# Attention context computed transposed, with the softmax division on the probabilities, in a fused layer on one core

## The reference

```python
q = split_heads(x @ wq + bq); k = split_heads(x @ wk + bk); v = split_heads(x @ wv + bv)
scores = jnp.einsum('bhqd,bhkd->bhqk', q, k) * dh ** -0.5 + attn_bias[:, None, :, :]
attn = jax.nn.softmax(scores, axis=-1)
ctx = jnp.einsum('bhij,bhjd->bhid', attn, v)          # 128 x 48 for each of 8 heads
attn_out = ctx.transpose(0, 2, 1, 3).reshape(b, n, d) @ wo + bo
x = _rmsnorm(x + attn_out, alpha1, gamma1)
x = _rmsnorm(x + silu(x @ w1 + b1) @ w2 + b2, alpha2, gamma2)
```

## Time and profile before

| What | Value |
|---|---|
| Median of 3 runs | 3255.15 us |
| Span of the profiled execution | 3262.2 us |
| TensorE matmul busy | 2983.9 us (91%) |
| TensorE weight loads busy | 2873.5 us (88%) |
| VectorE busy | 1913.3 us (59%) |
| ScalarE busy | 1531.1 us (47%) |
| GpSimd busy | 1444.8 us (44%) |
| Granted TensorE clock, mean | 0.970 |

### The profile page before, as it was taken

The page is one execution under the profiler, slowest core; times in us unless marked ns, Lnnn a source line. Parts: engine busy times, 40 slices in busy tenths (PEclk is TensorE's granted clock), DMA queues, the critical chain, the costliest instruction groups (busy, mean ns, idle before and its releaser), DMA issues. The chain is left out here.

```text
span 3262.2 us, 63713 instructions
## 1 busy us (share of the span) xinstructions
PE 2983.9 (91%) x21571; PEld 2873.5 (88%) x21571; DVE 1913.3 (59%) x3165; ACT 1531.1 (47%) x3966; POOL 1444.8 (44%) x1406
## 2 busy tenths in 40 slices
PE   3999999999999999999999847788899999999986
PEld 2899999999999999999999836688799999999982
DVE  4456556565656565565656447445577766666754
ACT  3454545545454545454454434355544544444530
POOL 0334444443434343444444347200377766666750
PEclk9999999999999999999999969889999999999999
DMA  3000101010101011010101057455566666666869
GB/s 122 28 23 31 36 24 43 24 43 24 43 24 43 23 35 32 24 43 24 43 24 39 20 209 282 137 154 164 185 209 215 210 187 186 210 194 189 260 225 365
DMA packets 293646, 358.96 MB, mean 110 GB/s; under 512 B 24328, under 2 KB 285960, under 8 KB 293512
## 3 DMA queue, kind: packets, MB, share of 16 engines
q1 hardware_dynamic: 284840, 344.92, 33.0%
q10 hardware_dynamic: 8704, 12.58, 1.0%
HBM read 286.14 MB, written 71.30 MB: 110 GB/s over the span
## 5 line engine op out<-in xcount | busy, mean ns | idle before, releaser
L1607 PE MATMUL u_bank<-x_in,x_w 128*128 128x256 f32 x4608 | 584.1, 286 | 25.1 <-issue 19.5
L1607 PEld LDWEIGHTS u_bank<-x_in,x_w 128*128 128x128 f32 x4608 | 578.5, 195 | 26.5 <-issue 26.5
L925 POOL TENSOR_TENSOR hT_lo<-h_tmp,hT_hi 128x512 fp32r<-128x512 f32 x192 | 247.8, 1290 | 483.3 <-DVE hT_hi L813 483.3
L1760 POOL TENSOR_TENSOR x_w<-raw,x_w 128x768 fp32r<-128x768 f32 x128 | 274.0, 2141 | 297.3 <-DVE x_w L1703 297.3
L1764 POOL TENSOR_TENSOR x_aT<-x_act,x_aT 128x512 fp32r<-128x512 f32 x128 | 299.5, 2339 | 212.0 <-ACT x_aT L1672 212.0
L389 PE MATMUL m_bank<-yT_hi,w_hi 128*128 128x256 f32 x1152 | 339.9, 295 | 0.0
L1663 ACT ACTIVATE x_gelu<-u_bank,x_b1T 128x256 f32<-128x256 f32 x256 | 121.9, 476 | 439.3 <-PE u_bank L1607 439.3
L389 PE MATMUL m_bank<-yT_lo,w_hi 128*128 128x256 f32 x1152 | 324.5, 282 | 0.0
L389 PE MATMUL m_bank<-yT_hi,w_lo 128*128 128x256 f32 x1152 | 323.9, 281 | 0.0
L660 ACT ACTIVATE h_tmp<-m_bank,b1c 128x256 f32<-128x256 f32 x384 | 160.9, 470 | 330.2 <-PE m_bank L389 329.8
L1619 PE MATMUL o_bank<-x_w,x_aT 128*128 128x384 f32 x1536 | 287.9, 335 | 1.8 <-POOL x_aT L1764 1.8
(11 more groups left out here) (212 smaller groups left out, 7408.8 us busy)
## 6 DMA issues: line engine op xcount, KB each, us to landing
raw<-in_L_ffn_w_dram SPq DMA_DIRECT2D x384, 384.0 KB, 5.1
ws_raw<-in_L_ffn_w_slot_dram SPq DMA_DIRECT2D x8, 2304.0 KB, 9.6
x_in<-in_x_dram SPq DMA_DIRECT2D x32, 384.0 KB, 3.4
x_res<-in_x_dram SPq DMA_DIRECT2D x32, 384.0 KB, 4.1
residual<-f_sb SPq DMA_DIRECT2D x32, 384.0 KB, 2.5
yn<-yn_sb SPq DMA_DIRECT2D x32, 384.0 KB, 2.5
yk<-yn SPq DMA_DIRECT2D x16, 768.0 KB, 11.2
se<-se SPq DMA_DIRECT2D x16, 768.0 KB, 3.3
```

Of the source, the lines that this page charges most:

```text
L925: nc.gpsimd.tensor_tensor(hT[i % 3][1][:], h_tmp[i % 2][:], hT[i % 3][0][:].bitcast(F32), ALU.subtract).then_inc(hl.sem, 1)
L1607: mm = pe.matmul(u_bank[n % BANKS][:, g, :], w1s[i % 2][a][:, c, g, c2 * P:(c2 + 1) * P], xT[e % 2][b][:, c, :], start=c == 0 and j == 0, ...
L1760: nc.gpsimd.tensor_tensor(w2s[i % 2][1][:], raw2[i][:], w2s[i % 2][0][:].bitcast(F32), ALU.subtract).then_inc(w2_lo.sem, 1)
```

## The change

Context is computed transposed. For each head the weights are now the head's values, padded with zeros from 48 to 64 columns (`v_sb` becomes `[P, GT, H, HP]`), and the probabilities in `pT` are streamed, 128 columns. The result of a head of par 0 goes to partitions 0 to 63 of the bank, that of par 1 to 64 to 127, and the two are issued in turn. The bank then already holds the transposed context, in four blocks of 128 padded rows. `context_T`, `ctx_sb` and VectorE's `context` are gone. `wo` is laid out to match (four chunks with zero rows), so `project_out` issues 12 matmuls in place of 9, and `cT` has 512 columns in place of 384.

The division is now made on the probabilities: VectorE `normalise` multiplies the 1024 columns of `s_sb[t]` by the reciprocals in place, and `prob_T` waits for that (`pn_ok`) in place of the exponentials.

`comb` becomes the same memory as `logit`, and so ScalarE's `comb_exp` also waits for `logits_T`. Scratch outputs of the squares move into other tiles. The bank uses are renumbered (20 in place of 22). TensorE now issues `project_out(a,0)` right behind `up(m,2)`, then `context(a,1)`, `up(m,3)`, `weights_T`. VectorE issues the statistics of the next group ahead of `recips` and `normalise`, and `row_max` behind them.

```diff
-    wo_s = split_pair("wo", [P, DC, D])
+    wo_s = split_pair("wo", [P, H // 2, D])
...
+            elif i == 3:
+                flat = s[:, 0:H // 2 * D]
+                srcs = [(flat[HP * par:HP * par + DH, :].rearrange("p (m f) -> p m f", f=D),
+                         w.rearrange("(m two e) f -> two e m f", two=2, e=DH)[par]) for par in range(2)]
...
+                    if i == 3:
+                        sp.wait_ge(zeroed.sem, 3)
...
+                nc.vector.memset(stage[3][:], 0.0).then_inc(zeroed.sem, 1)
...
-    comb = t_sb("comb", [P, GT, P])
+    comb = logit
...
             def prob_T(g, t):
+                pe.wait_ge(pn_ok.sem, pn_ok.at(g, t + 1))
                 for par in range(2):
-                    pe.wait_ge(p_ok.sem, p_ok.at(g, 8 * t + 4 * (par + 1)))
...
             def context(g, t):
                 pe.wait_ge(v_ok.sem, v_ok.at(g, t + 1))
-                held, k = ((sc_ok, 4), (pt_ok, 3))[t]
-                pe.wait_ge(held.sem, held.at(g, k))
+                if t == 0:
+                    pe.wait_ge(sc_ok.sem, sc_ok.at(g, 4))
+                pe.wait_ge(pt_ok.sem, pt_ok.at(g, 2 * t + 2))
                 bank = A_BANK[U_CTX[t]]
-                for par in range(2):
-                    pe.wait_ge(pt_ok.sem, pt_ok.at(g, 2 * t + par + 1))
-                    for m in range(H // 2):
-                        h = 2 * m + par
-                        mm = pe.matmul(bank[:, h * DH:(h + 1) * DH], pT[:, par, m, :],
-                                       v_sb[:, t, h * DH:(h + 1) * DH], start=True, stop=True)
-                mm.then_inc(a_full.sem, 1)
+                for m in range(H // 2):
+                    for par in range(2):
+                        mm = pe.matmul(bank[par * HP:(par + 1) * HP, tok(m)], v_sb[:, t, 2 * m + par, :],
+                                       pT[:, par, m, :], start=True, stop=True)
                 mm.then_inc(a_full.sem, 1)
...
             def project_out(g, t):
                 pe.wait_ge(cl.sem, cl.at(g, t + 1))
...
+                split_mm(bank[:, 0:D], [[cT[s][:, c, :] for s in range(2)] for c in range(H // 2)],
+                         [[wo_s[s][:, c, :] for s in range(2)] for c in range(H // 2)]).then_inc(a_full.sem, 1)
...
                 if M: up(m, 2)
-                if A: context_T(a, 0); context(a, 1)
+                if A: project_out(a, 0); context(a, 1)
                 if M: up(m, 3)
-                if A: project_out(a, 0); context_T(a, 1)
                 if R: weights_T(r)
...
+            def hi_cT(g, t):
+                act.wait_ge(a_full.sem, a_full.at(g, U_CTX[t] + 1))
+                nc.scalar.copy(cT[0][:], A_BANK[U_CTX[t]][:].rearrange("p (c n) -> p c n", n=P)).then_inc(ch.sem, 1)
...
             def comb_exp(g):
                 act.wait_ge(lm_ok.sem, lm_ok.at(g, 1))
+                act.wait_ge(r_full.sem, r_full.at(g, 4))
...
-                if A: hi_T(a, 0, U_CT, cT[0][:], ch)
-                if M: silu(m, 2); silu(m, 3)
-                if A: hi_T(a, 1, U_CT, cT[0][:], ch)
+                if A: hi_cT(a, 0)
+                if M: silu(m, 2)
+                if A: hi_cT(a, 1)
+                if M: silu(m, 3)
...
+            def lo_cT(g, t):
+                dve.wait_ge(ch.sem, ch.at(g, t + 1))
+                nc.vector.tensor_tensor(cT[1][:], A_BANK[U_CTX[t]][:].rearrange("p (c n) -> p c n", n=P),
+                                        cT[0][:].bitcast(F32), ALU.subtract).then_inc(cl.sem, 1)
...
+            def normalise(g, t):
                 dve.wait_ge(rs_ok.sem, rs_ok.at(g, t + 1))
...
+                rows_of = s_sb[t][:].rearrange("p a m n -> p (a m) n")
+                nc.vector.tensor_tensor(rows_of, rows_of, rsum[:, t, :].unsqueeze(2).broadcast_to([P, H, P]),
+                                        ALU.mult).then_inc(pn_ok.sem, 1)
...
-                if A: values(a, 0); values(a, 1); scores(a, 0); scores(a, 1); recips(a, 0)
+                if A: values(a, 0); values(a, 1); scores(a, 0); scores(a, 1)
                 if N: norm_stats(n, x_landed, 16, x_in, st, mv, stats, meanvar)
-                if R: row_max(r)
-                if A: context(a, 0); recips(a, 1)
-                if R: slot_max(r); comb_norm(r)
-                if A: lo_T(a, 0, U_CT, cT[0][:], cT[1][:], ch, cl)
+                if A: recips(a, 0); normalise(a, 0); recips(a, 1); normalise(a, 1)
+                if R: row_max(r); slot_max(r); comb_norm(r)
+                if A: lo_cT(a, 0)
                 if R: disp_recip(r)
                 if M: h_hi(m, 2)
-                if A: context(a, 1)
+                if A: residual(a, 0); lo_cT(a, 1)
                 if M: h_hi(m, 3)
-                if A: residual(a, 0); lo_T(a, 1, U_CT, cT[0][:], cT[1][:], ch, cl)
...
+            nc.vector.memset(v_sb[:], 0.0)
             run(dve, body)
```

More of the change, by code:

```diff
@@ L198, in _ @@
                 small_load(sp, rows["g2"][:], f_gamma2.rearrange("k (o d) -> k o d", o=1).broadcast_to([E1, S1, D]))
-                sp.wait_ge(zeroed.sem, 3)
+                sp.wait_ge(zeroed.sem, 4)
                 for n, b in enumerate((bq, bk)):
@@ L264, in setup_and_layer @@
     kT = t_sb("kT", [P, H // 2, GN])
-    v_sb = t_sb("v_sb", [P, GT, D])
+    v_sb = t_sb("v_sb", [P, GT, H, HP])
     s_sb = [t_sb(f"s_sb{t}", [P, 2, H // 2, P]) for t in range(GT)]
     pT = t_sb("pT", [P, 2, H // 2, P])
-    ctx_sb = t_sb("ctx_sb", [P, D])
-    cT = [t_sb("cT_hi", [P, DC, P], F32R), t_sb("cT_lo", [P, DC, P], F32R)]
+    cT = [t_sb("cT_hi", [P, H // 2, P], F32R), t_sb("cT_lo", [P, H // 2, P], F32R)]
     y = t_sb("y", [P, GT, D])
@@ L283, in setup_and_layer @@
     yn = t_sb("yn_sb", [P, GT, D])
-    squares = {n: t_sb("squares_" + n, [P, GT, D], BF16) for n in ("r", "f")}
     counts = t_sb("counts", [P, GT])
@@ L337, in setup_and_layer @@
     U_Q, U_K, U_V, U_S = (0, 1), (2, 3), (4, 5), ((6, 7), (8, 9))
-    U_PT, U_CTX, U_CT, U_WO, U_YT = ((10, 11), (13, 14)), (12, 16), (15, 18), (17, 19), (20, 21)
-    A_BANK = [a_bank[u % 3] for u in range(20)] + [a_bank[0], a_bank[2]]
-    ZT_BANK = [a_bank[2], a_bank[1]]
+    U_PT, U_CTX, U_WO, U_YT = ((10, 11), (13, 14)), (12, 16), (15, 17), (18, 19)
+    A_BANK = [a_bank[u % 3] for u in range(18)] + [a_bank[0], a_bank[1]]
+    ZT_BANK = [a_bank[1], a_bank[2]]
     def tok(t):
@@ L395, in zT_step @@
                 if past(g, 1):
-                    pe.wait_ge(r_ok.sem, r_ok.at(g - 1, t + 1))
+                    held, k = ((cl, 2), (r_ok, 2))[t]
+                    pe.wait_ge(held.sem, held.at(g - 1, k))
                 for c in range(DC):
@@ L405, in project @@
                         pe.wait_ge(yl.sem, yl.at(g - 1, 1))
-                if w is wk_s and n == 0:
+                if w is wq_s and n == 1:
                     if past(g, 1):
@@ L473, in project_out @@
                 pe.wait_ge(cl.sem, cl.at(g, t + 1))
-                held, k = ((pt_ok, 4), (ctx_ok, 2))[t]
-                pe.wait_ge(held.sem, held.at(g, k))
+                if t:
+                    pe.wait_ge(pt_ok.sem, pt_ok.at(g, 4))
                 bank = A_BANK[U_WO[t]]
-                split_mm(bank[:, 0:D], [[cT[s][:, c, :] for s in range(2)] for c in range(DC)],
-                         [[wo_s[s][:, c, :] for s in range(2)] for c in range(DC)]).then_inc(a_full.sem, 1)
+                split_mm(bank[:, 0:D], [[cT[s][:, c, :] for s in range(2)] for c in range(H // 2)],
+                         [[wo_s[s][:, c, :] for s in range(2)] for c in range(H // 2)]).then_inc(a_full.sem, 1)
             def yT_step(g, t):
@@ L482, in yT_step @@
                 if t == 0:
-                    pe.wait_ge(cl.sem, cl.at(g, 2))
+                    pe.wait_ge(r_ok.sem, r_ok.at(g, 1))
                 elif not (isinstance(g, int) and g == NG - 1):
@@ L632, in prob_T @@
                 if t:
-                    act.wait_ge(ctx_ok.sem, ctx_ok.at(g, t))
+                    act.wait_ge(a_full.sem, a_full.at(g, U_CTX[0] + 1))
                 else:
                     if past(g, 1):
-                        act.wait_ge(ctx_ok.sem, ctx_ok.at(g - 1, 2))
+                        act.wait_ge(a_full.sem, a_full.at(g - 1, U_CTX[1] + 1))
                 for par in range(2):
@@ L644, in square @@
                 act.wait_ge(sig_in.sem, sig_in.at(g, t + 1))
-                out, rows_in = squares[name][:, t, :] if name in squares else None, src[:, t, :]
+                out, rows_in = pT[:, t, :, :].rearrange("p m n -> p (m n)").bitcast(BF16)[:, 0:D], src[:, t, :]
+                if name == "r":
+                    out = s_sb[t][:].rearrange("p a m n -> p (a m n)").bitcast(BF16)[:, 0:D]
                 if name == "z":
@@ L762, in values @@
                 dve.wait_ge(a_full.sem, a_full.at(g, U_V[t] + 1))
-                nc.vector.tensor_tensor(v_sb[:, t, :], A_BANK[U_V[t]][:, 0:D], rows["bv"][:], ALU.add).then_inc(v_ok.sem, 1)
+                nc.vector.tensor_tensor(v_sb[:, t, :, 0:DH], A_BANK[U_V[t]][:, 0:D].rearrange("p (h e) -> p h e", h=H),
```

(13 more changed lines are left out.)

13 lines of the change are left out of this document (3 added, 10 removed).

## The result

The changed kernel takes 3401.74 us, the median of 4 runs (3398.32 to 3406.17), against 3253.48 us for the kernel before in the same runs: 1.0468 times as long, 95% interval 1.0439 to 1.0496. The profiled execution has a span of 3396.5 us. The forecast was 3418 us, slower.

What follows compares the result with a forecast made beforehand. TensorE's queue was taken to bound the kernel. Matmuls (-0.9) and two waits (+2.2, +2.1) gave +3.4 us per group, 109 us; clock falls added 54 us: 3418 us against the median, range 3340 to 3485 us.

Steps and rivals of the forecast that it cites:

- Matmuls that go and come: TensorE's work: transposes -0.66, `project_out` +1.05, contexts with halves side by side -1.3; together -0.9 us per group.
- First wait: At `prob_T(a,0)`, TensorE stands for VectorE's statistics, reciprocal and `normalise`; +2.2 us per group (2.0 to 2.6).
- Second wait: At `project_out(a,0)`, TensorE stands for the split context behind ScalarE's chain after `logits_T`; +2.1 us per group (1.5 to 2.4).
- What costs nothing: Other VectorE and ScalarE work, and the chain from `residual` to `yT_step`, claimed hidden; setup under 2 us once.
- The sum: Matmuls and both waits per group: -0.9 + 2.2 + 2.1 = +3.4 us, 109 us over 32 groups.
- The clock: Clock falls behind both new waits, 1.3 us each, at six in seven and two in five; +1.7 us per group, 54 us.
- Rival 4: Faster: TensorE takes later, ready work ahead of waiting transposes and `project_out`, filling both stalls; 3226 us, chance 0.10.
- Rival 2: Stalls as forecast, but the context's array halves run one after the other; 3475 us, or 3421 without falls; chance 0.20.
- Rival 1: Stalls as forecast, but the clock stays up in the layer; 3364 us, chance 0.16.
- Rival 3: Only one of the two stalls shows; +1.3 us per group, 3297 us without falls, chance 0.05.

Runs made afterwards that it cites:

- e_best3: Changed kernel with `comb` its own tile and TensorE reordered: ready feed-forward steps and the logits issued ahead of waiting steps; 3199.63 us, ratio 0.9837 to before.
- e_division_only: Kernel before with only the division changed: `normalise` ahead of `prob_T`, context merely copied out, statistics first on VectorE; 3321.53 us, ratio 1.0226 to before.
- e_comb_own: Changed kernel with `comb` a tile of its own again and `comb_exp` without its wait for `logits_T`; 3340.89 us, ratio 1.0296 to before.
- e_wo_later: Changed kernel with `project_out(a,0)` moved behind `up(m,3)` and `context(a,1)` ahead of it; 3315.81 us, ratio 1.0205 to before.
- e_down_first: Changed kernel with `down(m,1)` issued ahead of `prob_T(a,0)` instead of behind the logits; 3314.88 us, ratio 1.0195 to before.
- e_halves_apart: Changed kernel with the context's even heads all issued before the odd ones, not in turn; 3418.98 us, ratio 1.0535 to before.
- e_filled: Changed kernel with 13 added useless matmuls ahead of `prob_T(a,0)`'s wait for the normalised probabilities; 3337.04 us, ratio 1.0280 to before.

## Why the prediction was right

Slower was right, with a measured time within the range. By its steps, each from the place in the iteration at which TensorE's steps start (before 728.71, after 843.46 at the scores of block 0):

- **Matmuls that go and come.** Predicted -0.9 us per group, and right. The contexts hold the queue for 2 x 1.03 us in place of 3.50 us, and entering one costs 0.09 us more than the usual 0.174 us. With -0.66 for the transposes and +1.05 for `project_out` that is -0.66 + 1.05 - (3.50 - 2.06) + 0.18 = -0.87 us. e_best3 bears it out: 55.97 - 54.47 = 1.50 us, of which 0.70 is the old wait and 0.8 the work. The pair of halves side by side, which no row of before showed for columns, was the right end of the bound. The Trainium skill's ratio of 2.38 in 3 ("TensorE: Matmul & The Clock Gate", Part 3) gave 1.33 us a block with entering and leaving; measured in the same way are 1.12 us, where the prediction took 1.1.
- **First wait.** Predicted +2.2 us. The logits start 9.79 us after the scores and not 7.82: +1.97 us. The chain was as written: statistics, reciprocal, `normalise` in 1.23 us (1.25 taken). The reciprocal started about 0.2 us sooner, as successive instructions of an engine overlap a little at their ends in the trace (in rows 6 the bar from 742.81 ends at 743.89, and the next starts at 743.77); adding whole bars counted that twice. e_division_only shows the cause alone.
- **Second wait.** Predicted +2.1 us; 1.69 us idle, 1.84 us from start to start. The chain was right link by link; from the start of `prob_T(a,1)` to that of `project_out(a,0)` it took 5.14 us and not 5.4, for the same reason. What was read wrong later, in the expectation of e_comb_own, is what `comb_exp`'s wait costs: not the step's own 0.8 us but 1.28 us, since without it ScalarE need not wait for `logits_T` at all.
- **What costs nothing.** This step failed in part: its term for the chain behind `residual` was put at nothing, and it costs 0.46 us. `down(m,5)` starts late for GpSimd's low part of h (the 0.2 us of idle time in the profile hide the rest under the bar before it). The trace shows where that comes from:

```profile
865.43 0.56 DVE L799 TENSOR_TENSOR y<-a_bank,z 128x384 f32<-128x384 f32 x1 [0.65 <-PE a_bank L394]
868.71 0.84 ACT L661 ACTIVATE h_tmp<-m_bank,b1c 128x256 f32<-128x256 f32 x2 [1.75 <-PE m_bank L394]
870.18 1.45 POOL L925 TENSOR_TENSOR hT_lo<-h_tmp,hT_hi 128x512 fp32r<-128x512 f32 x1 [4.04 <-DVE hT_hi L814]
871.59 1.01 POOL L930 TENSOR_TENSOR y<-y,row_bo 128x384 f32<-128x384 f32 x1
```

GpSimd adds the bias to the first block's result (L930) only behind its low part of h for `up(m,3)`. The sum that it needs is ready at 865.99, but `up(m,3)` now comes behind `project_out(a,0)` and `context(a,1)`, and so GpSimd stands idle for 4.04 us and starts the addition 5.6 us late. Before the change it was 0.5 us (751.75 to 752.25):

```profile
751.19 0.56 DVE L798 TENSOR_TENSOR y<-a_bank,z 128x384 f32<-128x384 f32 x1 [0.27 <-PE a_bank L389]
752.25 1.01 POOL L930 TENSOR_TENSOR y<-y,row_bo 128x384 f32<-128x384 f32 x1
```

The delay runs on through the squares, `y_scale` and `residual(a,1)` to the last low part of h. ScalarE's and VectorE's new orders do not make it: `silu(m,3)` waited for TensorE, as the row at 868.71 says. e_wo_later, with `up(m,3)` in front again, has no such wait. No run moves GpSimd's order alone.
- **The sum.** +3.4 us predicted, +3.54 measured: 1.97 + 1.84 + 0.46 - 0.87 = 3.40. The other 0.14 us lie in the first matmul behind the second wait (0.28 us and not 0.174 to the next) and in transposes behind the new context. That the sum is so near is in part luck: a wait that was left out, and two waits taken 0.2 to 0.3 us too long, cancelled.
- **The clock.** The mechanism was right, both terms of the size were off. A fall costs 1.6 us, not the 1.3 taken from rows 7 and 8. Those counted only the eighteen matmuls; the three transposes ahead of them took 0.55 us from start to start, against 0.30 us in the one case without a fall, which would have made it about 1.6:

```profile
1960.27 0.55 PE L1057 MATMUL rt_bank<-ident,mean 128*128 128x128 f32 x3 [2.87 <-POOL mean L1166]
1960.57 3.37 PE L1073 MATMUL rs_bank<-ws,mT 128*128 128x384 f32 x18
```

The first wait had 23 falls in 29 (0.79, 0.86 forecast); the second, put at two in five, had none: in e_down_first it stands without the first, 1.69 us in every iteration, and the clock stays up. 23 x 1.6 = 38 us against 54 us predicted. That is about the 16 us between forecast and result: with the measured terms, 3255 + 32 x 3.54 + 38 = 3406 us, against 3402 us.

Rival 4, that TensorE would take ready work ahead of a waiting step, is excluded by e_down_first: the same instructions, issued ahead of the wait, fill it; behind it, they had not. Rival 2, halves one after the other, is excluded by the bars of e_halves_apart. Rival 1, the clock staying up, is what e_filled shows as a kernel: 59.5 us in every iteration. Rival 3, a single stall, falls by the two waits of the changed kernel's own rows.

## What to carry to other kernels

A step that is moved onto a queue's critical operand (here a division ahead of a transpose) costs its own length and the wait for its inputs, once for each place where the bounding engine has no other work issued in front; look for that work first and issue it ahead. Sharing a tile makes two chains one: a 0.8 us step that waits for another engine held everything queued behind it. An engine that is idle most of the time can still pass a delay on, if its queue holds a step that waits for work which was moved back. When work is saved on the bounding engine, redo its order: nearly the same instructions (`comb` apart) gave 4.7% slower and 1.6% faster.

## What the runs showed of the hardware

- Two halves of the array, 64 columns each, run float32 passes side by side when heads alternate: sixteen passes in 1.03 us, 0.064 us each, against 0.112 us with 128 weight columns. Apart, their bar is 1.58 us. The first of them starts 0.27 us behind the matmul before it (0.174 us is usual), and the step behind them 0.20 us after the last pass starts (0.109 us is usual): about 0.1 us each for entering and leaving.
- How many falls of the clock an idle stretch brings depends on more than the stretch. The wait is 2.46 to 2.47 us in five kernels, and behind it came falls in 23, 17, 16, 4 and 4 of 29 iterations (iterations of 59.51, 60.50, 57.14, 58.22 and 57.83 us). In the changed kernel, falls came in four or five successive iterations and then left one out. Why the count follows the iteration so was not tested and stays open.
- Most falls cost 1.6 us here: 61.14 - 59.51, 62.13 - 60.50, 59.84 - 58.22 and 58.75 - 57.14 us. Some cost 1.4 us: all four of e_division_only (59.25 - 57.83), six of e_halves_apart (61.91 - 60.50) and four of e_wo_later (58.53 - 57.14).
- An idle stretch of 1.69 us brought no fall in e_down_first, where no longer one stands in the iteration.
